# A fused image filter, text transformer and fusion network on one core: neighbour rows by transfers, a freed PSUM bank, norms scaled by ScalarE

## Chip, core and metric

The kernel runs on one core of a Trainium2 chip. Its time is device time in microseconds, the median of some runs. A profile is one execution of the program, recorded by the hardware; its span runs from the first to the last recorded instruction. The engines are TensorE (PE; its weight loads are PEld), VectorE (DVE), ScalarE (ACT), GpSimd (POOL) and the sync engine (SP), which here issues the transfers. Each runs its own instruction stream in order and meets the others at semaphores.

## What is computed

Three parts, all in float32. The first filters eight 256x256 images in ten iterations each, with differences to the right and lower neighbour and back:

```python
u = sigmoid(o / 0.5); q = 0
for _ in range(10):
    q = max(q - 0.5 * ((u_below - u) * vf1 + (u_right - u) * vf0), 0)
    Tq = (vf1*q - above(vf1*q)) + (vf0*q - left(vf0*q))
    u = sigmoid((o - Tq) / 0.5)
image_tokens = (o - Tq) / 0.5          # 256 tokens of 256 features
```

The second is a text transformer: 8 sequences of 128 tokens, width 256, four layers, each with 16-head attention, an output projection, a layer norm, a feed-forward pair 256 to 1024 to 256 with relu, and a second layer norm:

```python
h = layernorm(h + attention(h) @ wc) * g1 + e1
h = layernorm(h + relu(h @ w1 + b1) @ w2 + b2) * g2 + e2
```

The third joins both to 384 tokens per sample and applies windowed attention with a sink to the layer norm of the sum, adds it, then adds spike counts of a squared-relu feed-forward (256 to 1024 to 256) of a second layer norm.

## The kernel before

Engines are programmed by hand: one function per engine, with the order of all work written out, and semaphores between them. There are three stages.

*Text.* Samples go in pairs, so that four layers by four pairs make 16 blocks. `block_step(a, f, it)` runs the attention of block `a` beside the output projection, norm and feed-forward of block `f = a - 1`, and two filter iterations `it` and `it + 1`. `first_step` has attention of block 0 alone and two iterations. In PE's order the block starts with `carry_attn` (the residual put into PSUM by identity matmuls), `scores(a, 0)`, `project_out(f)`, `values(a)`, then `turn_probs`/`attend` in four parts among `ff1(f, 0..3)`, `carry_ffn`, and `ff2` in eight parts. `ff1` (L588) writes each quarter of the hidden layer to the one bank `ps_t[:, 0]`, and waits from the second quarter on until ACT's `hidden_out` has read the quarter before. The norms after `project_out` and `ff2` are `moments_*` (DVE, bn_stats L1557, bn_aggr L1560), `scale_of` (POOL: add epsilon L402, power L404), and `plain_rows` (DVE, two instructions at L1576).

*Fusion.* `fuse_first` handles sample 0 beside the last feed-forward of the text and two iterations; `fuse_step(n)` for n = 1 to 4 runs attention of sample n beside the feed-forward of n - 1 and two or one iteration; `fuse_late(n)` for n = 5 to 7 has no iteration, and `fuse_last` is the feed-forward of sample 7. On DVE are also `copy_text` (L1666), `norm_x` and `norm_y` (three instructions each at L1662) and `values_biased` (L1682).

*The filter iteration.* Two images lie over the 128 partitions, four image rows in each (`u`, `p1`: 4 rows of 256). DVE takes `differences` (L1507 inner rows, L1508 columns, L1511), `last_row` (L1515, L1516), `advance` (L1519, L1520), `flux_cols` (L1526), `flux_rows` (L1523), `inner_divergence` (L1532, L1533) and `divergence` (L1537, L1538, L1539). The row below the fourth and the one above the first lie in the next or the previous partition. PE brings them with a shift matrix: `rows_below` (L469) after ACT's tanh (`filter_out`, L997), `rows_above` (L473) after `flux_rows`. They lie in the PSUM bank `halo`. 32 of the 40 iterations run in the text stage, 8 in the fusion stage.

SP loads the weights of layer l + 1 when the last block of layer l has used the tile, and the images and all fusion weights at the start.

```python
    def ff1(k, j):
        ...
        else:
            pe_.wait_ge(s["act_ff1"], 4 * k + j)
        for m in range(2 * j, 2 * j + 2):
            for c in range(KC):
                last = mm(ps_t[:, 0, D * (m % 2):D * (m % 2) + D], w1[:, c, P * m:P * m + P], hT_f[:, c], ...)
```

## Time and profile before

| | us |
|---|---|
| median of 3 runs | 1062.35 (1060.9 to 1063.59) |
| the profiled execution's own time | 1059.45 |
| its span | 1057.5 |
| start to the end of `first_step` | 57.9 |
| 14 blocks, k = 1 to 14 | 555.9 |
| block 15 | 43.4 |
| `fuse_first` | 53.9 |
| `fuse_step` 1 to 4 | 187.2 |
| `fuse_late` 5 to 7, `fuse_last` | 128.6, 30.6 |

The text stages are cut where DVE ends the second `normalise` of a block (L1553), the fusion stages where PE ends `fuse_values`. A row of a window gives its length, then for each engine the busy time and number of instructions, the granted clock of TensorE as a share of full speed, and the transfers. The busy time of PE is modelled, and cannot be read as the time that its work needs at its peak.

### The profile page before, as it was taken

How to read it: one execution, taken by the hardware profiler on the slowest of the kernel's cores; microseconds unless marked ns; L12 is line 12 of the kernel's file. 1: busy time of each engine (PE TensorE's matmuls, PEld its weight loads, DVE VectorE, ACT ScalarE, POOL GpSimd, SP SyncE). 2: the span in 40 equal slices, each digit the busy share in tenths (PEclk: the TensorE clock that was granted, in tenths of full speed). 3: DMA queues.
4: the chain of work that ended last, by engine and by line, in shares of the span. 5: the costliest groups of instructions: out<-in, count | busy, mean ns of one | idle time of the engine just before them, and what ended most of it. 6: DMA issues, size and time to landing. Idle time of an engine off the chain costs nothing.

```text
span 1057.5 us, 18395 instructions
## 1 busy us (share of the span) xinstructions
PE 945.2 (89%) x6972; PEld 714.7 (68%) x6992; DVE 900.7 (85%) x1318; ACT 636.8 (60%) x2105; POOL 87.9 (8%) x149
## 2 busy tenths in 40 slices
PE   3589999889889989989989988789998999999997
PEld 2367777667667767767767766566666766667675
DVE  4999999999999999999999999798699699543542
ACT  1666667766666666666766665446455564745633
POOL 6100010001010010010010001010000001000000
PEclk9799999999999999999999999999999999999999
DMA  7600000110000110000110000000000000100000
GB/s 162 244 1 2 1 30 6 46 61 1 1 31 11 43 39 21 1 31 11 46 55 2 1 21 2 1 11 2 26 1 26 9 18 1 46 25 2 16 1 30
DMA packets 13544, 28.67 MB, mean 27 GB/s; under 512 B 2704, under 2 KB 9232, under 8 KB 12176
## 3 DMA queue, kind: packets, MB, share of 16 engines
q1 hardware_dynamic: 13072, 26.44, 7.5%
q0 software_dynamic: 384, 1.05, 0.6%
q8 instruction: 56, 0.92, 0.4%
q14 instruction: 32, 0.26, 0.1%
HBM read 22.25 MB, written 5.24 MB: 26 GB/s over the span
## 4 chain that ended last, share of the span: by engine, by line
PE 45%; DVE 43%; ACT 7%; issue 4%; DMA 1%; SPq 0%; POOL 0%; POOLq 0%; ACTq 0%; DVEq 0%
PE ps_t L595 8%; PE ps_t L604 7%; PE ps_s L493 4%; DVE neg_max L1544 4%; PE ps_m L808 3%; PE ps_t L797 3%; DVE f L1538 2%; DVE f L1520 2%; DVE f L1516 2%; DVE f L1519 2%; DVE p L1526 2%; DVE f L1511 2%; DVE p L1523 2%; DVE f L1508 2%; DVE f L1533 2%
## 5 line engine op out<-in xcount | busy, mean ns | idle before, releaser
L1010 ACT ACTIVATE prob<-ps_s,neg_max 128x128 f32<-128x128 f32 x512 | 180.1, 379 | 52.2 <-DVE neg_max L1544 52.2
L595 PE MATMUL ps_t<-hT_f,w 128*128 128x256 f32 x512 | 133.0, 404 | 33.1 <-ACT hT_f L1022 17.2
L595 PEld LDWEIGHTS ps_t<-hT_f,w 128*128 128x128 f32 x512 | 95.3, 196 | 58.9 <-ACT hidT L1076 23.9
L1018 ACT ACTIVATE probT<-ps_t 128x512 f32<-128x512 f32 x128 | 77.2, 603 | 83.2 <-PE ps_t L554 52.6
L604 PE MATMUL ps_t<-w,hidT 128*128 128x256 f32 x512 | 125.4, 383 | 0.0
L1010 ACT ACTIVATION_READ_ACCUMULATOR prob<-ps_s,neg_max 128x1 f32 x512 | 112.8, 220 | 0.0
L604 PEld LDWEIGHTS ps_t<-w,hidT 128*128 128x128 f32 x512 | 91.1, 190 | 12.2 <-issue 3.0
L797 PE MATMUL ps_t<-km,w_fc 128*128 128x384 f32 x256 | 94.4, 504 | 1.7 <-ACT km L1183 1.0
L554 PE MATMUL ps_t<-ident,prob 128*128 128x128 f32 x512 | 81.4, 283 | 5.9 <-ACT prob L1010 3.7
L1076 ACT ACTIVATE hidT<-ps_t,b 128x256 f32<-128x256 f32 x128 | 54.8, 491 | 49.8 <-PE ps_t L595 49.8
L554 PEld LDWEIGHTS ps_t<-ident,prob 128*128 128x128 f32 x512 | 63.0, 145 | 28.4 <-issue 11.8
L1544 DVE TENSOR_REDUCE neg_max<-ps_s 128x8 f32<-128x1024 f32 x64 | 76.0, 1210 | 2.9 <-PE ps_s L544 2.9
L1215 ACT ACTIVATE prob<-ps_s,neg_max 128x128 f32<-128x128 f32 x192 | 54.0, 380 | 29.3 <-DVE neg_max L1688 29.3
L493 PE MATMUL ps_s<-hT_a,w_attn 128*128 128x256 f32 x256 | 65.3, 401 | 3.0 <-ACT hT_a L1022 2.3
L808 PE MATMUL ps_m<-w_pr,o_all 128*128 128x256 f32 x256 | 66.1, 385 | 0.0
L797 PEld LDWEIGHTS ps_t<-km,w_fc 128*128 128x128 f32 x256 | 46.4, 193 | 27.4 <-issue 3.9
L493 PEld LDWEIGHTS ps_s<-hT_a,w_attn 128*128 128x128 f32 x256 | 48.5, 200 | 12.1 <-ACT hT_a L1022 5.1
L1520 DVE TENSOR_TENSOR f<-f 128x1024 f32<-128x1024 f32 x40 | 50.0, 1251 | 1.4
L808 PEld LDWEIGHTS ps_m<-w_pr,o_all 128*128 128x128 f32 x256 | 45.7, 190 | 7.4
L1519 DVE SCALAR_TENSOR_TENSOR f<-f 128x1024 f32<-128x1024 f32 x40 | 49.3, 1231 | 1.1
L1538 DVE TENSOR_TENSOR f<-f 128x1024 f32<-128x1024 f32 x40 | 49.0, 1225 | 1.4
L1516 DVE TENSOR_TENSOR f<-f,vf 128x1024 f32<-128x1024 f32 x40 | 49.0, 1225 | 1.4
(172 smaller groups left out, 1879.3 us busy)
## 6 DMA issues: line engine op xcount, KB each, us to landing
w<-in_w SPq DMA_DIRECT2D x8, 1024.0 KB, 4.9
w_attn<-in_w_attn SPq DMA_DIRECT2D x4, 768.0 KB, 4.6
out<-w SPq DMA_DIRECT2D x7, 384.0 KB, 2.4
o_all<-in_o SPq DMA_DIRECT2D x4, 512.0 KB, 10.5
filtered<-f_out SPq DMA_DIRECT2D x4, 512.0 KB, 2.6
x<-filtered SPq DMA_DIRECT2D x8, 256.0 KB, 2.7
vf<-in_vf SPq DMA_DIRECT2D x4, 256.0 KB
w_attn<-in_w_attn SPq DMA_DIRECT2D x4, 256.0 KB, 3.1
```

The costliest lines, as they stand in the source:

```text
L493: last = mm(dst, w_attn[:, c, D * w + P * m:D * w + P * m + P], hT_a[:, k % 2, c], start=(c == 0), stop=(c == KC - 1))
L554: last = tr(ps_t[:, 1, P * hh:P * hh + P], prob[:, n % 2, 4 * half + hh], ident[:])
L595: last = mm(ps_t[:, 0, D * (m % 2):D * (m % 2) + D], w1[:, c, P * m:P * m + P], hT_f[:, c], start=(c == 0), stop=(c == KC - 1))
L604: last = mm(ps_t[:, 0, D * t:D * t + D], hidT[:, m, P * t:P * t + P], w2[:, m], start=False, stop=(m == MC - 1), skip_group_check=True)
L797: last = mm(ps_t[:, m % 2, 0:TOK], w_fc[:, c, P * m:P * m + P], xn2T[:, c], start=(c == 0), stop=(c == KC - 1))
L808: last = mm(dst, hid_f[:, m, P * t:P * t + P], w_pr[:, m], start=(m == 0), stop=(m == MC - 1))
L1010: last = A(prob[:, n % 2, hh], ps_s[n % 2][:, hh], ACT.Exp, scale=-1.0, bias=neg_max[:, n % 2, hh:hh + 1], accum_out=den)
L1018: A(probT[:, 4 * half:4 * half + 4].rearrange("p h k -> p (h k)"), ps_t[:, 1], ACT.Copy).then_inc(s["act_pT"], 1)
L1516: link(tt(fa, fa, vf[:, 0], ALU.mult))
L1519: link(stt(q_st, q_st, 0.0, fa, ALU.max, ALU.subtract))
L1520: link(tt(q_st, q_st, fb, ALU.subtract))
L1544: dve.tensor_reduce(neg_max[:, n % 2], ps_s[n % 2][:], AX.X, ALU.min).then_inc(s["dve_max"], 1)
```

## The change

The iterations per block become a list: one in block 0 and in block 15, two in the others, so 30 in text; `fuse_first` and all four `fuse_step` have two. `u` gets a fifth row below and `p1` a fifth row above; SP fills them by two SBUF to SBUF transfers each (63 partitions of 1 KB, one per image), and the two PE functions, the shift matrices and the bank `halo` go. The differences across rows become one instruction over 1024 elements, where there had been one of 768 and one of 256. SP's loads are spread through the blocks among these transfers.

The freed bank, `ps_y` (`row_bank`), takes the residual and output projection and `turn_ffn`; `ff1` alternates between it and `ps_t[:, 0]`. The norms are scaled by ACT, as `scale * x + shift`, for which POOL also makes `-mean` and `-mean * rstd` (two small instructions more for each norm). The exceptions are the last layer's second norm and sample 0's first norm, which stay on DVE. ACT also takes `copy_text` and the copy of the window values; the value bias is added in `values_in`. The orders of PE, ACT and DVE are rewritten in all stages: among others the second `head_max` of a block follows `flux_rows`, and `scores(a, 1)` comes behind three quarters of `ff1`.

```diff
-ITERS_IN_BLOCK = 2
-TEXT_ITERS = ITERS_IN_BLOCK * BLOCKS
-FUSE_ITERS = [2, 1, 2, 1, 2, 0, 0, 0]
+BLOCK_ITERS = [1, 2, 2, 2, 2, 2, 2, 2, 2, 2, 2, 2, 2, 2, 2, 1]
+TEXT_ITERS = sum(BLOCK_ITERS)
+FUSE_ITERS = [2, 2, 2, 2, 2, 0, 0, 0]
...
-        u = sb("u", [P, RPP, IMG + 1])
+        u = sb("u", [P, RPP + 1, IMG + 1])
-        p1 = sb("p1", [P, RPP, IMG])
+        p1 = sb("p1", [P, RPP + 1, IMG])
-        halo = ps("halo", [P, 2, IMG])
+        ps_y = ps("ps_y", [P, 2, D])
+        row_bank = ps_y[:, :, :].rearrange("p t n -> p (t n)")
+        ff_banks = [ps_t[:, 0], row_bank]
...
+            def rows_below(it):
+                if it < ITERS * PAIRS:
+                    sp.wait_ge(s["act_tanh"], it + 1)
+                    for at in (0, 64):
+                        sp.dma_start(u[at:at + 63, RPP, 0:IMG], u[at + 1:at + 64, 0, 0:IMG]).then_inc(s["halo_u"], 16)
+
+            def rows_above(it):
+                sp.wait_ge(s["dve_flux"], it + 1)
+                for at in (0, 64):
+                    sp.dma_start(p1[at + 1:at + 64, 0], p1[at:at + 63, RPP]).then_inc(s["halo_p"], 16)
...
+            rows_below(0)
+            for k in range(BLOCKS):
+                it, its, l = sum(BLOCK_ITERS[:k]), BLOCK_ITERS[k], k // PAIRS
+                for i in range(its):
+                    rows_above(it + i)
+                    if i == 0 and k < PAIRS - 1:
+                        load_images(k + 1).then_inc(s["l_img_rest"], 16)
+                    if i == 0 and k % PAIRS == PAIRS - 1 and l + 1 < LAYERS:
+                        load_projections(l + 1)
+                    if i == 0 and k % PAIRS == 0 and l:
+                        load_out(l)
+                    if i == 1 and k % PAIRS == 0 and l:
+                        load_ff_in(l)
+                    rows_below(it + i + 1)
+                    pair_done(it + i)
...
             def scale_attn(k):
-                scale_of(s["dve_stat_a"], s["pool_eps_a"], k, mv_a, var_eps_a, rstd_a, s["pool_rstd_a"])
+                pool.wait_ge(s["dve_stat_a"], k + 1)
+                if k:
+                    pool.wait_ge(s["act_ln1"], k)
+                pool.tensor_tensor(var_eps_a[:], mv_a[:, :, 1], eps_c[:, 0:2], ALU.add).then_inc(s["pool_eps_a"], 1)
+                pool.tensor_tensor(neg_mean_a[:], mv_a[:, :, 0], minus[:, 0:2], ALU.mult).then_inc(s["pool_eps_a"], 1)
+                pool.wait_ge(s["pool_eps_a"], 2 * k + 2)
+                pool.tensor_tensor(rstd_a[:], var_eps_a[:], pow_half[:, 0:2], ALU.pow).then_inc(s["pool_rstd_a"], 1)
+                pool.wait_ge(s["pool_rstd_a"], k + 1)
+                pool.tensor_tensor(shift_a[:], neg_mean_a[:], rstd_a[:], ALU.mult).then_inc(s["pool_shift_a"], 1)
...
-            def rows_below(it):
-                pe_.wait_ge(s["act_tanh"], it + 1)
-                mm(halo[:, 0], up_shift[:], u[:, 0, 0:IMG], start=True, stop=True).then_inc(s["pe_halo"], 1)
...
             def ff1(k, j):
...
-                else:
-                    pe_.wait_ge(s["act_ff1"], 4 * k + j)
+                    if k:
+                        pe_.wait_ge(s["h_ready"], 4 + k)
+                elif j >= 2:
+                    pe_.wait_ge(s["act_ff1"], 4 * k + j - 1)
                 for m in range(2 * j, 2 * j + 2):
                     for c in range(KC):
-                        last = mm(ps_t[:, 0, D * (m % 2):D * (m % 2) + D], w1[:, c, P * m:P * m + P], hT_f[:, c], start=(c == 0), stop=(c == KC - 1))
+                        last = mm(ff_banks[j % 2][:, D * (m % 2):D * (m % 2) + D], w1[:, c, P * m:P * m + P], hT_f[:, c], start=(c == 0), stop=(c == KC - 1))
...
-            def block_step(a, f, it):
+            def block_step(a, f, it, its):
                 carry_attn(f)
                 scores(a, 0)
                 project_out(f)
                 values(a)
-                rows_below(it)
                 turn_probs(a, 0, 0)
                 turn_ffn(f)
                 ff1(f, 0)
                 turn_probs(a, 0, 1)
                 ff1(f, 1)
-                rows_above(it)
+                ff1(f, 2)
+                attend(a, 0)
+                turn_probs(a, 1, 0)
                 scores(a, 1)
...
+            def scaled_rows(k, bank, rstd_, shift_):
+                hp = h[:, 2 * (k % PAIRS):2 * (k % PAIRS) + 2]
+                for t in range(2):
+                    last = A(hp[:, t], bank[:, D * t:D * t + D], ACT.Identity, scale=rstd_[:, t:t + 1], bias=shift_[:, t:t + 1])
+                return last
...
             def block_step(a, f, it, its):
                 exps(a, 0, 0)
-                exps(a, 0, 1)
+                values_out(a)
+                norm_attn(f)
                 probs_out(a, 0, 0)
                 ffn_in(f)
+                exps(a, 0, 1)
+                hidden_out(f, 0)
...
-            def last_row(it):
-                dve.wait_ge(s["pe_halo"], 2 * it + 1)
-                link(stt(fa[:, RPP - 1], halo[:, 0], edge[:], u[:, RPP - 1, 0:IMG], ALU.add, ALU.subtract))
+            def differences_down(it):
+                dve.wait_ge(s["halo_u"], 32 * it + 32)
+                link(tt(fa, u[:, 1:, 0:IMG], u[:, 0:RPP, 0:IMG], ALU.subtract))
                 link(tt(fa, fa, vf[:, 0], ALU.mult))
...
             def divergence(it):
-                dve.wait_ge(s["pe_halo"], 2 * it + 2)
-                link(tt(fa[:, 0], p1[:, 0], halo[:, 1], ALU.subtract))
+                dve.wait_ge(s["dve_flux"], it + 1)
+                dve.wait_ge(s["halo_p"], 32 * it + 32)
+                link(tt(fa, p1[:, 1:], p1[:, 0:RPP], ALU.subtract))
                 link(tt(fa, fa, fb, ALU.add))
                 stt(fa, o_all[:, it // ITERS], 4.0, fa, ALU.mult, ALU.subtract).then_inc(s["dve_div"], 1)
...
-            def block_step(a, f, it):
-                differences(it)
+            def block_step(a, f, it, its):
+                differences_across(it)
                 head_max(a, 0)
                 moments_attn(f)
+                differences_down(it)
+                advance(it)
+                flux_rows(it)
                 head_max(a, 1)
-                norm_attn(f)
-                last_row(it)
-                advance(it)
                 flux_cols(it)
-                flux_rows(it)
-                inner_divergence(it)
+                divergence_across(it)
                 divergence(it)
                 head_max(a, 2)
                 head_max(a, 3)
...
+                if its > 1:
+                    differences_across(it + 1)
+                    differences_down(it + 1)
+                    advance(it + 1)
...
+                if its > 1:
+                    flux_rows(it + 1)
+                    flux_cols(it + 1)
                 reciprocals(a, 0)
...
+                    divergence_across(it + 1)
+                reciprocals(a, 1)
                 moments_ffn(f)
-                reciprocals(a, 1)
-                divergence(it + 1)
-                norm_ffn(f)
+                if its > 1:
+                    divergence(it + 1)
                 normalise(a, 0)
                 normalise(a, 1)
```

## Rows read from the trace of the kernel before

**Rows 1.** The page's first part: busy us, share of the span, instructions.
```profile
PE 945.2 (89%) x6972; PEld 714.7 (68%) x6992; DVE 900.7 (85%) x1318; ACT 636.8 (60%) x2105; POOL 87.9 (8%) x149
```

**Rows 2.** Windows: stretch, length, busy PE, PEld, DVE, ACT, POOL, clock, transfers.
```profile
22.00:57.93 35.93, 23.82 (x167) 16.04 (x166) 32.40 (x34) 20.96 (x86) 8.45 (x13) 0.76 0.56 199
57.93:613.80 555.87, 513.08 (x3648) 405.13 (x3648) 539.84 (x679) 378.29 (x1389) 39.55 (x70) 0.99 0.06 21
613.80:657.23 43.43, 35.16 (x257) 26.84 (x255) 42.47 (x64) 27.51 (x100) 5.46 (x7) 1.00 0.03 11
657.23:711.10 53.87, 45.11 (x370) 34.31 (x373) 46.94 (x82) 22.55 (x57) 6.40 (x9) 0.97 0.02 6
711.10:898.30 187.20, 176.24 (x1416) 124.57 (x1424) 160.47 (x278) 102.67 (x262) 10.48 (x16) 1.00 0.04 12
898.30:1026.90 128.60, 122.10 (x1017) 86.54 (x1026) 57.98 (x139) 70.78 (x188) 5.21 (x10) 1.00 0.06 19
...
296.52:335.68 39.16, 36.12 (x262) 28.54 (x261) 38.25 (x49) 26.83 (x100) 2.82 (x5) 1.00 0.07 21
```

**Rows 3.** Groups by line: shapes, count, busy us, mean ns, idle before.
```profile
L1532 DVE TENSOR_TENSOR f<-p 128x768 f32<-128x768 f32 x40 | 38.3, 957 | 1.2
...
L1507 DVE TENSOR_TENSOR f<-u 128x768 f32<-128x768 f32 x40 | 37.1, 927 | 2.6 <-ACT u L997 2.6
...
L1515 DVE SCALAR_TENSOR_TENSOR f<-halo,edge,u 128x256 f32<-128x256 f32 x40 | 19.0, 475 | 0.0
...
L1022 ACT ACTIVATE hT_f<-ps_t,cols 128x256 f32<-128x256 f32 x32 | 16.3, 560 | 10.7 <-PE ps_t L478 10.7
L1576 DVE TENSOR_SCALAR h<-ps_t,mv_a,rstd_a 128x256 f32<-128x256 f32 x32 | 15.9, 539 | 0.8 <-POOL rstd_a L404 0.2
L1537 DVE TENSOR_TENSOR f<-p,halo 128x256 f32<-128x256 f32 x40 | 15.9, 398 | 0.9 <-PE halo L473 0.3
...
L1662 DVE TENSOR_SCALAR km<-x,mv_x,rstd_x 128x256 f32<-128x256 f32 x24 | 8.4, 407 | 0.1
```

**Rows 4.** Timeline within one steady block: start, duration, engine, line.
```profile
318.58 0.59 PE L469 MATMUL halo<-u,up_shift 128*128 128x256 f32 x2
...
331.52 0.70 POOL L404 TENSOR_TENSOR rstd<-var_eps,pow_half 128x2 f32<-128x2 f32 x1
331.62 1.23 DVE L1538 TENSOR_TENSOR f<-f 128x1024 f32<-128x1024 f32 x1
...
332.88 1.23 DVE L1539 SCALAR_TENSOR_TENSOR f<-o_all,f 128x1024 f32<-128x1024 f32 x1
...
334.02 0.99 DVE L1576 TENSOR_SCALAR h<-ps_t,mv,rstd 128x256 f32<-128x256 f32 x2
334.13 1.06 ACT L997 ACTIVATE u<-f 128x1024 f32<-128x1024 f32 x1
334.93 0.41 DVE L1553 TENSOR_TENSOR attnT<-ps_m,rden 128x256 f32<-128x256 f32 x1
...
335.59 0.94 DVE L1507 TENSOR_TENSOR f<-u 128x768 f32<-128x768 f32 x1
```

**Rows 5.** Transfers: count, KB each, median us from issue to landing.
```profile
w<-in_w SPq DMA_DIRECT2D x8, 1024.0 KB, 4.9
...
x<-filtered SPq DMA_DIRECT2D x8, 256.0 KB, 2.7
...
out<-w SPq DMA_DIRECT2D x1, 128.0 KB, 1.7
```

**Rows 6.** PE's waits in blocks 1 to 14: total us, times, longest.
```profile
PE ps_t L595 <- ACT hidT L1076: 13.6, 26, 0.6
PE ps_t L478 <- DVE h L1576: 10.5, 14, 0.9
```

**Rows 7.** Timeline in `fuse_first`: a POOL instruction and the DVE one beside it.
```profile
674.27 1.04 POOL L419 TENSOR_TENSOR hT_r<-hT_f,cols 128x512 f32<-128x512 f32 x1 [3.46 <-ACT hT_f L1022]
...
674.45 1.95 DVE L1520 TENSOR_TENSOR f<-f 128x1024 f32<-128x1024 f32 x1
```

More of the change, by code:

```diff
@@ L494, in project, with carry @@
                 return last
[L496 removed]
+            def carry(bank, src):
                 for t in range(2):
@@ L1646, in first_step @@
                 reciprocals(0, 0)
-                differences(1)
-                last_row(1)
-                advance(1)
-                flux_cols(1)
-                flux_rows(1)
-                inner_divergence(1)
                 reciprocals(0, 1)
-                divergence(1)
                 normalise(0, 0)
```

734 lines of the change are left out of this document (374 added, 360 removed).

## The prediction

> **What bounds the kernel now.** I read the page's shares first: PE is busy 89% of the span and DVE 85% [rows 1], so the whole page cannot say which of them sets the time. The windows can [rows 2]. In blocks 1 to 14 DVE is busy 539.84 of 555.87 us, 97%; PE 513.08, 92%; ACT 68%. A steady block has 39.16 us with 38.25 of DVE. What is left to DVE there, 0.9 us, is spread over some 49 instructions and is the gap between linked ones. So DVE sets the text stage, and PE, which waits in small pieces for ACT and DVE [rows 6], is close behind it. In `fuse_step` 1 to 4 the order is reversed: PE 176.24 of 187.2 us, 94%, DVE 160.47, 86%. In `fuse_late` PE is busy 95% and DVE 45%: there is room for filter work on DVE in the fusion stage, and none in the text stage. Block 15 (42.47 of 43.43) and `first_step` from 22 us on (32.40 of 35.93) are DVE's too.
>
> **Part 1: rows by transfers, on DVE.** Across rows, 927 + 475 = 1402 ns [rows 3] become one instruction of 1024 elements, about 1225 as L1538 and L1539 take [rows 4]. Back across rows, 957 + 398 = 1355 become 1225. Instructions of which the second does not wait overlap by some 0.06 us, so that of 0.31 us per iteration I count 0.18: 0.36 us per block.
>
> **Part 2: the norms.** DVE loses two pairs of L1576 per block. A pair takes from 334.02 to 334.93, 0.91 us [rows 4]; two make 1.82. ACT gains four instructions of 560 ns, of the form of L1022 (scale and bias from PSUM, the same 128x256) [rows 3], about 2.0 us, on 26.83 of 39.16. That is hidden: the first pair lies where ACT waits for the first maximum and the second behind the queries' copy, before the next exponentials. POOL's two more instructions, each some 0.2 us, lengthen the chain moments to `ff1(f, 0)` by 0.3 to 0.5 us; DVE no longer delays that chain, and ACT may (it must finish four exponentials and the values' copy first). PE's wait for this norm is 0.75 us per block now [rows 6]; I expect 1.2.
>
> **A new wait.** Today L1576 stands between the last divergence and the next differences and covers the tanh. L1539 ends at 334.11, the tanh runs 334.13 to 335.19, and DVE goes on at 335.59 without a gap [rows 4]. After the change only `normalise` stands there, 335.59 - 334.93 = 0.66 us, against 1.1 to 1.2 us from the end of the divergence to the end of the tanh. DVE stalls 0.45 us per block; the first exponentials' maximum is queued behind it, and ACT and PE's `turn_probs` wait for that.
>
> A steady block on DVE: 39.16 - 0.36 - 1.82 + 0.45 = 37.4 us, 1.75 less. 14 blocks: **-24.5 us**.
>
> **Part 3: does PE follow?** PE loses four shift matmuls per block of 0.59 us each [rows 4], 2.4 us, and the wait of `ff1` for `hidden_out`, about 1.0 us [rows 6]. 36.12 - 2.4 = 33.8 busy; with the 5% of idle that `fuse_late`, a PE-bound stage, has [rows 2], 35.5. By the chain instead of the share: 39.16 less 2.4 and 1.0, plus 0.5 for the norm, is 36.3. POOL's `hT_r`, on which `carry_ffn` waits, follows the first divergence (17.8 us into the block by DVE's sum) and takes 1.04 us [rows 7], soon enough for a `carry_ffn` at about 20. So PE lies at 35.5 to 36.3 and DVE stays the bound, by 1 us. The freed bank and the matmuls alone bring nothing in this stage; they are what lets PE follow.
>
> **Part 4: are the transfers hidden?** The trace has no SBUF to SBUF transfer. The nearest rows are 1.7 us from issue to landing for 128 KB and 2.7 for 256 KB; 4.9 for 1 MB is the upper end [rows 5]. SP issues two per halo, some 0.45 us apart, so from the releasing instruction to both landed I take 0.1 + 0.45 + 1.7 to 2.7 = 2.3 to 3.3 us (63 KB is nearest to the 128 KB row); at most 5.5. The covers on DVE: from `flux_rows` to the divergence in the first half `head_max`, `flux_cols` and the differences across, 3.6 us; in the second 3.8; from tanh to `differences_down` in the first half two differences, a maximum and the moments, 4.6 us; in the second half the maxima hide the tanh and 3.6 us remain. All four are longer than 3.3: the transfers cost nothing, and everything beyond 3.6 us would cost up to four times per block. SP's order puts the 1 MB loads right behind a halo, with 8 us or more to the next. SP waits for weights (`pe_v`, `pe_wc`, `pe_ff1`, `pe_ff2`) that are reached before the halo queued behind them.
>
> The Trainium skill speaks against this form: "DMA: Bandwidth & Descriptors", section "Rules for kernel authors", says that two transfers to disjoint partition halves serialize and that one should be used, and its section on the anatomy of a DMA gives a fixed 2.0 us plus bytes at 436 GB/s. If the second waited for the whole of the first, that would be an estimated 4.3 us by the page; the trace of before has no such pair to agree or disagree. What it would do here is the second rival.
>
> **Part 5: the moved iterations.** One iteration is 15 us of DVE. Block 15 has 42.47 us of DVE [rows 2]; less 15, less the norm, it falls to some 26, and PE's 35 decides with its waits: 43.4 to 36.5, **-6.9 us**. `first_step` loses an iteration too, 17 us of DVE remain of 32.4, but its attention chain stays: the second maximum now comes behind `flux_rows`, 6 us later than today, so the exponentials of the second part start later and PE and ACT (23.82 and 20.96 us busy, clock 0.76) are left to run almost in series. The gain lies between 0 and 35.93 - 23.82 = 12 us; I take **-3.5**, near the lower end for that order.
>
> `fuse_first`: DVE loses 0.9 (norm), six instructions of 407 ns (`norm_x`, `norm_y`) [rows 3], some 0.8 (copy and values, two instructions near L1537's 0.4) and 0.4 (rows), so 46.94 becomes 42.4; PE loses four shift matmuls, 2.4, and starts its queries without waiting for block 15's DVE. Of 53.87 I take **-6.0**: 48, which leaves PE (42.7) its present share of waits. Bounds 0 and -9.
>
> `fuse_step` 1 to 4: DVE 160.47 + 2 x 15 - 8 x 0.2 - 4 x 3.3 = 175.7, 43.9 per step; PE 176.24 - 12 x 0.59 = 169.2, 42.3 per step, 44.4 with its 5%. The two are now almost equal, so 45.5 per step: 182 for 187.2, **-5.2**. Bounds -10 and +8. Here the transfers have longer covers, since maxima and normalisations stand between. `fuse_late` and the tail: PE-bound, DVE's work moved to ACT (70.78 of 128.6): 0.
>
> The Trainium skill's page "SBUF — State Buffer", section "SBUF: two separate sides", says that a GpSimd instruction and a DVE instruction with two SBUF inputs hold a shared port pair exclusively. The trace agrees for a large one: L1520 takes 1.95 us beside POOL's hT_r, in place of 1.23 [rows 7, 4]. It does not for a small one: L1538 takes 1.23 beside the power of 0.70 us [rows 4]. If each of the two new small ones cost DVE its 0.2 us, 30 text norms would add 12 us; I count nothing.
>
> **The sum.** -24.5 - 6.9 - 3.5 - 6.0 - 5.2 = -46.1: the span goes from 1057.5 to 1011.4; with 1.95 us around it (1059.45 - 1057.5) 1013.4. That is the profiled execution. The median of the runs shown is 2.9 us above it, so 1016.
>
> **The rivals.**
> 1. *Another engine's order becomes the bound.* The norm goes through ACT, whose order is rigid: when four exponentials are late, `norm_attn`, `turn_ffn` and all of `ff1` are. For it: PE has only 1 us of room, and waits for this norm already. Against: 1.75 us of DVE leave the block. Blocks at 38.5 instead of 37.4: 1016 + 15 = 1031.
> 2. *Slower: the two halves of a halo run one after the other.* 2 x 2.3 = 4.6 us from release to landing, against covers of 3.6: 1.0 us for each of the 60 halos in the text stage, +60: 1076. It decides from 46 / 60 = 0.77 us of stall, at 4.4 us; between 4.2 and 4.4 nothing would change. Against: 16 engines share even 1 MB in 4.9 us, and one small transfer leaves them almost idle. This is what the skill's rule above would bring about.
> 3. *More is gained.* No tanh stall, blocks at PE's 36.2, `first_step` -8, steps at 44: 1016 - 17 - 4.5 - 6 = 988. For it: if the first maximum is not ready, the stall lies in a wait that exists anyway.
> 4. *The moved iterations are not hidden*, `fuse_step` at 48.5 as DVE and PE wait for each other: 1016 + 12 = 1028; it lies in the range.
>
> **Chances and range.** Forecast with its bounds (1000 to 1027) 0.60; rival 1 or 4, alone or together up to 1045, 0.19; rival 3, 0.13; within 0.3% by transfers of 4.2 to 4.4 us, 0.03; rival 2, 0.05. Of measurements I take 0.3% as what can be told from no change. Faster 0.92, same 0.03, slower 0.05. The range goes from rival 3 to rivals 1 and 4 together with a further 0.1 us per block: 986 to 1045.
>
> **What the profile after would show.** Part 1: DVE instructions of 1024 elements at 1.22 us, none of 768, and no wait for a transfer beyond 0.2 us; any idle of DVE before `differences_down` or `divergence` that ends with a landing contradicts part 4. Part 2: `norm` on ACT at about 0.56 us, and a DVE idle of some 0.45 us per block before the differences, ended by the tanh; if it isn't there, rival 3. Part 3: a steady block of 37.4 us with DVE at 36.5 busy, PE below 34.5; if PE's waits for ACT's h have grown over 1.5 us per block, rival 1. Part 5: block 15 near 36.5 us with DVE idle, steps near 45.5 with DVE near 44. The forecast is wrong if the block is not 37.4, since that term is more than half of it.

## The result, and the profile after

| us | before | after |
|---|---|---|
| median of the runs of this comparison | 1061.62 (1060.78 to 1063.59) | 1094.66 (1088.74 to 1100.5) |
| profiled execution, span | 1059.45, 1057.5 | 1100.5, 1098.8 |
| start to the end of `first_step` | 57.9 | 63.2 |
| blocks 1 to 14 | 555.9 | 581.2 |
| block 15 | 43.4 | 43.7 |
| fusion | 400.3 | 410.6 |

The changed kernel is slower: ratio 1.0308, 95% interval 1.0246 to 1.037. I had forecast 1016 us. Every stage misses its forecast: `first_step` by 8.8 us, blocks 1 to 14 by 49.8, block 15 by 7.2, fusion by 21.5. The profiled execution of the changed kernel is the longest of its four, 5.8 us above their median.

The page's first part after, to be held against [rows 1]:

```profile
PE 937.7 (85%) x6808; PEld 717.3 (65%) x6832; DVE 848.9 (77%) x1121; ACT 690.4 (63%) x2221; POOL 177.7 (16%) x244
```

The windows after, for [rows 2] (stretch, length, busy PE, PEld, DVE, ACT, POOL, clock, transfers); the last row is one steady block:

```profile
22.00:63.23 41.23, 23.17 (x167) 16.21 (x166) 18.08 (x20) 22.23 (x89) 6.37 (x13) 0.67 0.28 86
63.23:644.46 581.23, 504.27 (x3535) 402.26 (x3534) 509.98 (x568) 399.42 (x1438) 111.57 (x126) 0.92 0.12 39
644.46:688.18 43.72, 35.37 (x246) 27.21 (x244) 26.63 (x46) 28.11 (x101) 7.15 (x13) 0.87 0.07 22
688.18:1098.80 410.62, 369.79 (x2852) 267.59 (x2876) 285.65 (x466) 236.65 (x589) 40.13 (x69) 0.95 0.06 20
227.85:269.77 41.92, 36.57 (x258) 28.89 (x256) 37.06 (x42) 29.62 (x105) 7.98 (x9) 0.92 0.15 51
```

DVE did lose its work (539.8 to 510.0 us in the 14 blocks) and is now idle for 12% of them. Two columns stand out: POOL, from 39.6 to 111.6 us, far more than 28 times two short instructions; and PE's granted clock, from 0.99 to 0.92. The groups of POOL say where its time is (busy us and mean ns of one, then idle before):

```profile
L456 POOL TENSOR_TENSOR rstd_a<-var_eps_a,pow_half 128x2 f32<-128x2 f32 x16 | 24.8, 1551 | 1.3
L467 POOL TENSOR_TENSOR rstd<-var_eps,pow_half 128x2 f32<-128x2 f32 x16 | 23.2, 1450 | 1.3
L453 POOL TENSOR_TENSOR var_eps_a<-mv_a,eps_c 128x2 f32<-128x2 f32 x16 | 17.2, 1078 | 140.7 <-DVE mv_a L1665 140.7
```

The same instructions in the kernel before:

```profile
L404 POOL TENSOR_TENSOR rstd_a<-var_eps_a,pow_half 128x2 f32<-128x2 f32 x16 | 11.1, 695 | 1.3
L402 POOL TENSOR_TENSOR var_eps_a<-mv_a,eps_c 128x2 f32<-128x2 f32 x16 | 3.1, 195 | 182.3 <-DVE mv_a L1560 182.3
```

One steady block of the changed kernel in order of time shows what they meet (start, duration, then in brackets idle before and who ended it):

```profile
232.72 0.25 DVE L1665 BATCH_NORM_AGGREGATE mv_a<-stats_a 128x2 f32<-128x6 f32 x2
232.89 1.19 DVE L1621 TENSOR_TENSOR f<-u 128x1024 f32<-128x1024 f32 x1
233.05 1.08 POOL L453 TENSOR_TENSOR var_eps_a<-mv_a,eps_c 128x2 f32<-128x2 f32 x1 [5.81 <-DVE mv_a L1665]
234.12 1.25 DVE L1622 TENSOR_TENSOR f<-f,vf 128x1024 f32<-128x1024 f32 x1
234.37 1.55 POOL L456 TENSOR_TENSOR rstd_a<-var_eps_a,pow_half 128x2 f32<-128x2 f32 x1
235.99 0.68 POOL L458 TENSOR_TENSOR shift_a<-neg_mean_a,rstd_a 128x2 f32<-128x2 f32 x1
236.71 1.02 ACT L1095 ACTIVATE h<-ps_y,shift_a,rstd_a 128x256 f32<-128x256 f32 x2 [2.27 <-POOL shift_a L458]
237.79 1.12 PE L539 MATMUL ps_y<-ident,h 128*128 128x128 f32 x4 [3.60 <-ACT h L1095]
240.01 3.70 PE L658 MATMUL ps_t<-hT_f,w 128*128 128x256 f32 x8 [1.11 <-ACT hT_f L1065]
```

`var_eps_a` starts 0.16 us behind the start of L1621, a difference of two SBUF tensors, and ends 0.05 us after it, at 234.13 to 234.08. `rstd_a` starts inside L1622 and still runs for 0.55 of its usual 0.70 us after that one's end at 235.37. `shift_a` starts inside L1625 and ends 0.04 us after it. From the end of the moments to ACT's norm there are 3.7 us. In the kernel before there were 1.15, from 302.20 to 303.35:

```profile
301.95 0.25 DVE L1560 BATCH_NORM_AGGREGATE mv_a<-stats_a 128x2 f32<-128x6 f32 x2
303.35 1.00 DVE L1576 TENSOR_SCALAR h<-ps_t,mv_a,rstd_a 128x256 f32<-128x256 f32 x2
```

Of the 2.6 us between the two, the lengthening of `var_eps_a` and `rstd_a` is 0.88 and 0.86. `shift_a` takes 0.68 where its twin `neg_mean_a`, which starts 0.02 us ahead of L1622, takes 0.19; if that is its own time, 0.5 more is lengthening. That leaves some 0.4 us for the two added instructions themselves. PE stands still for 3.6 us and comes back at its lower level, 1.2 GHz: the first quarter of `ff1` takes 3.70 us, later quarters 1.89. The waits after, total, times, longest, for [rows 6]:

```profile
PE ps_y L539 <- ACT h L1095: 56.3, 16, 3.7
ACT h L1095 <- POOL shift_a L458: 37.8, 16, 3.3
DVE neg_max L1649 <- PE ps_s L605: 59.8, 16, 4.7
DVE f L1614 <- ACT u L1040: 5.5, 12, 0.5
DVE f L1621 <- DMA u<-u: 10.4, 6, 6.5
```

In the kernel before, the first of them was:

```profile
PE ps_t L478 <- DVE h L1576: 11.9, 16, 0.9
```

The longer wait of PE comes back to DVE as a wait for the next scores (59.8 us).

### The profile page after: what moved, and what is told of

The parts are those of the page before. It is cut to its first block, busy times and chain, and to the rows that moved or that the text cites. A ratio compares the mean times of both kernels' runs of the same rounds, so it can differ in the third digit from the quotient of the medians.

```text
span 1098.8 us, 18348 instructions
## 1 busy us (share of the span) xinstructions
PE 937.7 (85%) x6808; PEld 717.3 (65%) x6832; DVE 848.9 (77%) x1121; ACT 690.4 (63%) x2221; POOL 177.7 (16%) x244
## 4 chain that ended last, share of the span: by engine, by line
PE 34%; DVE 34%; ACT 12%; POOL 7%; issue 6%; DMA 4%; SPq 1%; POOLq 0%; ACTq 0%; DVEq 0%
PE ps_t L658 8%; PE ps_t L857 6%; DMA u<-u 4%; PE ps_y L658 3%; PE ps_s L804 2%; ACT u L1040 2%; PE ps_m L868 2%; DVE f L1643 2%; POOL rstd_a L456 2%; DVE f L1622 2%; DVE f L1626 2%; DVE f L1625 2%; DVE f L1621 2%; PE ps_t L615 2%; DVE f L1642 2%
## 5 line engine op out<-in xcount | busy, mean ns | idle before, releaser
L669 PE MATMUL ps_t<-w,hidT 128*128 128x256 f32 x512 | 129.2, 386 | 0.0
L1649 DVE TENSOR_REDUCE neg_max<-ps_s 128x8 f32<-128x1024 f32 x64 | 76.7, 1219 | 59.8 <-PE ps_s L605 59.8
L1053 ACT ACTIVATION_READ_ACCUMULATOR prob<-ps_s,neg_max 128x1 f32 x512 | 121.4, 237 | 0.0
L658 PE MATMUL ps_t<-hT_f,w 128*128 128x256 f32 x256 | 89.7, 512 | 16.8 <-ACT hT_f L1065 16.7
L615 PE MATMUL ps_t<-ident,prob 128*128 128x128 f32 x512 | 85.5, 293 | 17.6 <-ACT prob L1053 16.7
L615 PEld LDWEIGHTS ps_t<-ident,prob 128*128 128x128 f32 x512 | 63.3, 150 | 45.0 <-ACT prob L1053 25.2
L658 PEld LDWEIGHTS ps_t<-hT_f,w 128*128 128x128 f32 x256 | 64.6, 260 | 34.4 <-ACT hT_f L1065 22.3
L539 PE MATMUL ps_y<-ident,h 128*128 128x128 f32 x64 | 16.0, 397 | 56.3 <-ACT h L1095 56.3
L658 PE MATMUL ps_y<-hT_f,w 128*128 128x256 f32 x256 | 63.2, 391 | 0.0
L1305 ACT ACTIVATE prob<-ps_s,neg_max 128x128 f32<-128x128 f32 x192 | 53.9, 382 | 11.3 <-DVE neg_max L1773 11.3
L1772 DVE TENSOR_REDUCE rmax<-ps_s 128x4 f32<-128x512 f32 x48 | 33.0, 687 | 34.1 <-PE ps_s L804 33.8
L464 POOL TENSOR_TENSOR var_eps<-mv,eps_c 128x2 f32<-128x2 f32 x16 | 16.5, 1032 | 260.0 <-DVE mv L1665 260.0
L1621 DVE TENSOR_TENSOR f<-u 128x1024 f32<-128x1024 f32 x40 | 48.4, 1210 | 11.4 <-DMA u<-u 10.4
L1614 DVE TENSOR_TENSOR f<-u 128x1024 f32<-128x1024 f32 x40 | 48.6, 1214 | 5.5 <-ACT u L1040 5.5
```

What stands on the lines that cost most here:

```text
L615: last = tr(ps_t[:, 1, P * hh:P * hh + P], prob[:, n % 2, 4 * half + hh], ident[:])
L658: last = mm(ff_banks[j % 2][:, D * (m % 2):D * (m % 2) + D], w1[:, c, P * m:P * m + P], hT_f[:, c], start=(c == 0), stop=(c == KC - 1))
L669: last = mm(ps_t[:, 0, D * t:D * t + D], hidT[:, m, P * t:P * t + P], w2[:, m], start=False, stop=(m == MC - 1), skip_group_check=True)
L1053: last = A(prob[:, n % 2, hh], ps_s[n % 2][:, hh], ACT.Exp, scale=-1.0, bias=neg_max[:, n % 2, hh:hh + 1], accum_out=den)
L1305: last = A(prob[:, t % 2, head], quad[hb][:, P * hh:P * hh + P], ACT.Exp, bias=neg_max[:, t, head:head + 1])
L1614: link(tt(fb, u[:, 0:RPP, 1:], u[:, 0:RPP, 0:IMG], ALU.subtract))
```

## The experiments

My theory after the traces: POOL's short instructions of the norm are held by DVE's instructions with two SBUF inputs, since the change put those right behind the moments in place of the second maximum, which reads PSUM; the norm of the attention then reaches PE late, and PE's clock falls in the wait. I call this lengthening of POOL's instructions the hold; an exchange is the pair of transfers that brings one set of neighbour rows. The rivals were the late maximum, the norm's place on ACT, the transfers and the moved iterations. Each run was compared with runs of the kernel before made beside it, and its ratio is to those; `e5` and the like are the runs' names, and in the table each row from e2 on adds to the one above. The stages of the profiled runs, in us:

| | first | 1 to 14 | 15 | fusion | ratio of the runs |
|---|---|---|---|---|---|
| before | 57.9 | 555.9 | 43.4 | 400.3 | 1 |
| after | 63.2 | 581.2 | 43.7 | 410.6 | 1.031 |
| e2, maximum ahead | 63.3 | 567.0 | 41.7 | 406.6 | 1.012 |
| e1, and norm on DVE | 63.0 | 552.4 | 40.0 | 408.1 | 1.003 |
| e5, and first exchange early | 55.9 | 550.8 | 39.9 | 405.6 | 0.995 |

**e2: the second maximum directly behind the moments.**

```diff
                 moments_attn(f)
+                head_max(a, 1)
                 differences_down(it)
                 advance(it)
                 flux_rows(it)
-                head_max(a, 1)
```

> The changed kernel with one line moved in DVE's block_step: the second head_max comes directly behind moments_attn, as in the kernel before, ahead of differences_down. It reads PSUM only, so POOL's four small instructions get some 1.2 us in which DVE runs nothing with two SBUF inputs. Theory P (DVE's two-SBUF-input instructions hold POOL up, the norm's chain grows, PE idles and its clock falls): epsilon add of the attention norm back from 1.08 to 0.19 us, power from 1.55 to about 0.7, PE's wait for ACT's h from 3.7 to some 1.5 us per block, granted clock above 0.96, blocks of 38.5 to 39.5 in place of 41.5: 1050 to 1065 us. Rival T (transfers and SP's queue are the cost): nothing of that, 1090 to 1100. Rival O (the rigid order of ACT alone, with POOL's lengthening harmless): POOL's times fall, but the blocks stay above 41.

1078.38 us, ratio 1.0123 (1.0065 to 1.0182). POOL's groups in e2:

```profile
L458 POOL TENSOR_TENSOR shift_a<-neg_mean_a,rstd_a 128x2 f32<-128x2 f32 x16 | 15.3, 959 | 1.3
L456 POOL TENSOR_TENSOR rstd_a<-var_eps_a,pow_half 128x2 f32<-128x2 f32 x16 | 12.0, 748 | 1.3
L453 POOL TENSOR_TENSOR var_eps_a<-mv_a,eps_c 128x2 f32<-128x2 f32 x16 | 4.0, 250 | 140.6 <-DVE mv_a L1665 140.6
```

The two that now run beside a maximum from PSUM are back at 250 and 748 ns, and the one that reaches into the differences behind it has become longer, 959 ns. PE's wait for h falls from 56.3 to 35.4 us. The forecast on POOL held, the one on the time did not: PE still waits 2.2 us a block (forecast 1.5), the clock of the blocks stays at 0.92 (forecast above 0.96), a block takes 40.5 us and the run 13 us more than the top of the range. In one steady block there are still 2.3 us from the end of the moments to ACT's norm. This run moves the maximum too, so it does not part the two causes by its time; POOL's rows do for the port.

**e1: e2, and the attention norm on DVE again**; POOL makes only `rstd_a`, ACT's `norm_attn` is gone.

```diff
                 head_max(a, 1)
+                norm_attn(f)        # on DVE: ts(hp[:, t], rows[:, t], mv_a[:, t, 0:1], rstd_a[:, t:t + 1], ...)
                 differences_down(it)
```

> e2_max_first, and the attention norm of the text stage scaled on DVE again (two instructions behind the second head_max, POOL makes the factor only). P: PE's wait for h as before the change, 0.7 to 1.0 us per block, blocks near 38, clock 0.98: 1040 to 1055. If scaling on ACT as such is the cost, this is faster than e2_max_first by over 10 us; if only POOL's hold-up is, the two are within 5 us, since DVE gets 0.9 us more per block. T: 1090 to 1100.

1066.22 us, ratio 1.0025 (0.9998 to 1.0052); 12 us less than e2, which by my own rule means that scaling on ACT is a cost of its own. The run takes away POOL's `neg_mean_a` and the held `shift_a` together with ACT's norm, so it does not part these. PE's wait for h is 16.9 us, nearly as forecast; the time is above the forecast of 1040 to 1055, since a block takes 39.5 us and not 38.

**e3: the order of the change in the kernel before.**

```diff
+                last_row(it)
                 head_max(a, 1)
                 norm_attn(f)
-                last_row(it)
```

> The kernel before with two lines of DVE's block_step in reverse order: last_row (whose second instruction has two SBUF inputs) between moments_attn and the second head_max. No transfer, no norm on ACT. P: POOL's epsilon add or power for the attention norm, 0.19 and 0.70 us today, grows towards 1 to 1.5 us in every block where it meets L1516, and PE's wait for h grows; the norm itself comes 1.7 us later at most by DVE's order. 1065 to 1090 us. O and T: POOL's times as before, and 1062 to 1070 by the later norm.

1128.27 us, ratio 1.0601 (1.0556 to 1.0645). The time is far above the forecast, and the part on POOL missed: its instructions kept 197 and 696 ns, because nothing stood beside them. DVE waited there for PE's shift matmul:

```profile
328.29 0.25 DVE L1560 BATCH_NORM_AGGREGATE mv_a<-stats_a 128x2 f32<-128x6 f32 x2
328.89 0.69 POOL L404 TENSOR_TENSOR rstd_a<-var_eps_a,pow_half 128x2 f32<-128x2 f32 x1
329.65 0.48 DVE L1515 SCALAR_TENSOR_TENSOR f<-halo,edge,u 128x256 f32<-128x256 f32 x1 [1.11 <-PE halo L469]
332.57 0.99 DVE L1576 TENSOR_SCALAR h<-ps_t,mv_a,rstd_a 128x256 f32<-128x256 f32 x2
```

So the run says nothing on the hold. With that wait of 1.1 us and the two instructions of `last_row`, the maximum and the norm come 2.9 us later (4.0 us from the moments to the norm, for 1.15), and a block takes 44.2 us in place of 39.7: some 1.5 us for each microsecond of lateness.

**e9: the kernel before with the power computed twice**, so that this norm alone comes 0.7 to 0.8 us later.

```diff
+                pool.tensor_tensor(spare_a[:, 0:2], var_eps_a[:, 0:2], pow_half[:, 0:2], ALU.pow)...
                 pool.tensor_tensor(rstd_a[:, 0:2], var_eps_a[:, 0:2], pow_half[:, 0:2], ALU.pow)...
```

> The kernel before with POOL's power for the attention norm computed twice (0.7 us and a handover more, 16 times), so that the norm and only the norm comes 0.8 us later; DVE waits for it. If a late norm costs its delay, 16 x 0.8 = 13 us: 1073 to 1078. If it is amplified (PE's clock falls, and exponentials and scores are late in turn), 1085 to 1100. If the chain has slack, under 1068.

1084.4 us, ratio 1.0192 (1.0154 to 1.0229): 20 us for 16 x 0.8 = 13 us, blocks 41.3. PE's wait for h is 24.2 us (11.9 before), its clock 0.96. That lies between the two forecasts. The lateness of the norm alone, without the maximum, is paid in full and by half again.

**e6: the changed kernel, six matmuls whose result nobody reads in PE's wait for the norm.**

```diff
                 turn_probs(a, 0, 0)
+                if f:
+                    pe_.wait_ge(s["h_ready"], 4 + f)
+                for _ in range(6):
+                    mm(ps_t[:, 0, 0:D], ident[:], hT_a[:, a % 2, 0], start=True, stop=True)
                 turn_ffn(f)
```

> The changed kernel with six matmuls whose result nobody reads (into the free half of ps_t) between turn_probs(a, 0, 0) and turn_ffn, where PE waits 3.7 us per block for the norm. They take some 3 us of that wait. If the lower clock after that wait is a cost of its own (the four matmuls of ff1(f, 0) take 3.7 us after it, 2.0 elsewhere, granted clock 0.92), the clock returns to 0.98 or more, ff1(f, 0) to 2.0 us, and a block loses 1 to 1.7 us: 1070 to 1080. If the clock does not matter beside the chain, 1090 to 1100.

1074.97 us, ratio 1.0108 (1.0077 to 1.0139): 20 us less with more work. Clock in the 14 blocks 0.97 (0.92), and in the block's order:

```profile
233.30 0.66 PE L539 MATMUL ps_y<-ident,h 128*128 128x128 f32 x4 [1.01 <-ACT h L1099]
235.07 2.98 PE L658 MATMUL ps_t<-hT_f,w 128*128 128x256 f32 x8 [1.11 <-ACT hT_f L1069]
```

The same groups took 1.12 and 3.70 us in the changed kernel, 1.2 us more a block, or 18 us in 15 blocks; by the windows the 15 blocks give back 16.3 us. So about half of the loss against before was PE at 1.2 GHz behind a wait in which it did nothing. The rest, 4.6 us by the windows, came in the fusion stage.

**e4: the transfers alone in the kernel before**, with its order of work and its norms; among others:

```diff
-                link(stt(fa[:, RPP - 1], halo[:, 0], edge[:], u[:, RPP - 1, 0:IMG], ALU.add, ALU.subtract))
+                dve.wait_ge(s["halo_u"], 32 * it + 32)
+                link(tt(fa, u[:, 1:, 0:IMG], u[:, 0:RPP, 0:IMG], ALU.subtract))
...
-                link(tt(fa[:, 0], p1[:, 0], halo[:, 1], ALU.subtract))
+                dve.wait_ge(s["halo_p"], 32 * it + 32)
+                link(tt(fa, p1[:, 1:], p1[:, 0:RPP], ALU.subtract))
```

> The kernel before with the first part of the change alone: neighbour rows by two transfers each, one instruction across rows, the two shift matmuls and their bank gone, loads of layers spread among the transfers; images and fusion weights still loaded at the start. P: the transfers are hidden but for the first ones behind the loads, POOL's times as before: 1045 to 1062. T: DVE idles for landings, 1.3 us per block or more: 1080 to 1100.

1124.86 us, ratio 1.0566 (1.0519 to 1.0613), above both forecasts. VectorE's waits in e4:

```profile
DVE f L1582 <- DMA p<-p: 38.6, 33, 1.8
DVE f L1561 <- DMA u<-u: 20.1, 3, 18.7
```

In the order of before only 1.2 us of DVE's work lie between `flux_rows` and the instruction that needs its transfer. The change needs its new order to hide the transfers. 18.7 us is the first exchange alone, issued behind the loads of images and weights.

**e5: e1 with the first exchange issued ahead of the weights.**

```diff
+            sp.wait_ge(s["act_tanh"], 1)
+            for at in (0, 64):
+                sp.dma_start(u[at:at + 63, RPP, 0:IMG], u[at + 1:at + 64, 0, 0:IMG]).then_inc(s["halo_u"], 16)
             sp.wait_ge(s["g_emb"], 16 * (B - 2))
...
-            rows_below(0)
```

> e1_norm_dve with the two transfers of the first halo issued before SP's wait for the gathered rows, ahead of the weight loads. There its first halo landed while the loads ran, and DVE idled 7.3 us for it in first_step. If that wait is first_step's loss, first_step ends 4 to 6 us earlier and nothing else moves: 1060 to 1063 where e1_norm_dve had 1066. Rival: first_step is bound by its attention chain at the low clock, and it gains under 2 us.

1058.56 us, ratio 0.9949 (0.9924 to 0.9973). SP's queue in the changed kernel, and what DVE waits for behind it:

```profile
20.29 0.57 SPq L273 DMA_DIRECT2D w_attn<-in_w_attn  x1
...
22.98 0.43 SPq L278 DMA_DIRECT2D w<-in_w  x1
24.48 1.72 SPq L322 DMA_DIRECT2D u<-u  x2
...
33.21 1.23 DVE L1621 TENSOR_TENSOR f<-u 128x1024 f32<-128x1024 f32 x1 [6.54 <-DMA u<-u]
```

The exchange is issued behind six loads of weights, and DVE can go on only 8.7 us after SP began to issue it. e5 is the only version with all of the work in it that is ahead of the kernel before, by 0.5% (0.3 to 0.8), a small gain; it is 3% ahead of the changed kernel. `first_step` ends 7.1 us earlier than in e1, a little more than forecast.

**e8: e1 with the old distribution of the iterations**; the second iteration also goes back into `first_step` on DVE and ACT.

```diff
-BLOCK_ITERS = [1, 2, 2, 2, 2, 2, 2, 2, 2, 2, 2, 2, 2, 2, 2, 1]
-FUSE_ITERS = [2, 2, 2, 2, 2, 0, 0, 0]
+BLOCK_ITERS = [2] * 16
+FUSE_ITERS = [2, 1, 2, 1, 2, 0, 0, 0]
```

> e1_norm_dve with the iterations as before the change: two in each of the 16 blocks, 2, 1, 2, 1, 2 in the fusion steps. Prediction's part 5: first_step 3 to 8 us longer (a part of that is the late first halo in both), block 15 5 to 7 longer, the two steps with one iteration 1 to 3 us shorter each: 1072 to 1080 against 1066. Rival: the fusion stage pays for the moved iterations in full, and the time is within 0.3% of e1_norm_dve.

1066.79 us, ratio 1.0029 (1.0004 to 1.0053), e1 had 1066.22. Block 15 takes 43.8 us (40.0 in e1), the four fusion steps 189.6 (195 to 196 with all ten iterations; 184.9 before), `first_step` 2.7 more. These steps, and those of e10, are cut where DVE ends the second moments of a sample, and not as in the table before the change. The rival holds: the moves cancel. The two iterations are 6 us of the fusion steps' loss; the other 4.7 us, 189.6 against 184.9, are there without them, and no run here shows their cause.

**e10: e5 with the fusion stage's norms on DVE again**, at the places of the kernel before.

```diff
                 advance(it + 1)
+                norm_x(n + 1)
                 residual(n)
```

> The kernel of e5 with the two norms of the fusion stage back on VectorE, at the places where the kernel before has them. Fusion took 400.3 us before and 405.6 in e5, with two more filter iterations in it. Theory N (ScalarE stands still for GpSimd's shift_y and shift_x, 15.1 and 8.8 us in all in the changed kernel, and this is what fusion lost): fusion 400 to 403, 3 to 6 us less than e5, about 1053 to 1056. Theory I (the two added iterations are the loss; VectorE takes some 1.2 us more a norm and has no room in the steps with two iterations): fusion 405 to 412, 1058 to 1065.

1066.34 us, ratio 1.0046 (1.0012 to 1.008): fusion 412.7 us, a step 51.1 us instead of 48.8. That is theory I's side, 1 us above its bounds. Here the change's norm on ACT is right, by some 7 us.

**e7: each exchange as one transfer of 127 partitions; e11: of 126.**

```diff
-                for at in (0, 64):
-                    sp.dma_start(p1[at + 1:at + 64, 0], p1[at:at + 63, RPP]).then_inc(s["halo_p"], 16)
+                sp.dma_start(p1[1:128, 0], p1[0:127, RPP]).then_inc(s["halo_p"], 16)
```

> The kernel of e5 with each neighbour-row exchange as one transfer of 127 partitions in place of two of 63 (the row at the border between the two images is then wrong: the edge value is overwritten by the other image's row; all else is computed). SP took 0.72 us to issue each half, so the second half of every exchange started 0.72 us behind the first, and in e1's steady block VectorE waited 0.70 us for p<-p and 1.02 us for u<-u. Theory T (the second half ends what VectorE waits for, and VectorE is the bound of a block now): 0.7 us less at each wait that is there, 1.0 to 1.4 us a block, blocks 39.4 -> 38.2 to 38.6, in all 14 to 20 us less than e5: 1039 to 1045. Theory R (these waits lie beside TensorE's path, which ends the block): the waits shrink and the blocks stay within 0.3 us, 1054 to 1058.

> The kernel of e7 with 126 partitions in its one transfer in place of 127 (besides the row at the border between the two images, the last partition's neighbour row is not brought either; all else is computed). In e7 the one transfer of 127 rows was the slow thing: from the last flux instruction to its arrival 7.2 us (two halves of 63: 3.0 us), and while VectorE waited the DMA share was 0.06, one of 16 engines, at 17 GB/s. Theory D (127 rows can't be dealt out evenly, so one DMA engine carries them all; 126 can, over 9 or 14 engines): the one transfer takes 2.3 to 2.6 us, the waits of e5 (0.71 and 1.09 us in a block) shrink to about 0 and 0.4 us, blocks 39.4 -> 38.4, 1038 to 1047. Theory B (crossing partition 64, or the larger size, is slow in itself): as e7, 1300 us or more. If theory D holds for the transfer but TensorE ends the blocks: 1052 to 1057.

e7 took 1354.69 us, ratio 1.2742 (1.266 to 1.2825), e11 1051.66, ratio 0.9889 (0.9832 to 0.9945). The first two rows are waits of e7, the third a window of e7 in which DVE waits for u<-u:

```profile
DVE f L1632 <- DMA p<-p: 198.2, 40, 6.1
DVE f L1611 <- DMA u<-u: 92.4, 20, 4.9
...
431.90:436.61 4.71, 4.71 (x39) 3.60 (x38) 0.08 (x2) 1.73 (x10) 0.00 (x0) 0.93 0.06 17
```

The share is the mean over 16 DMA engines, so 0.06 is what one of them gives when it alone is busy. Counted from the end of the instruction that releases it, not from the later one that I had used in e11's text, the 127 rows took 8.4 us, the two halves 3.1 in e5, the 126 rows 2.6. e7's time is in neither of its two ranges. e11 decides for theory D, with the time as if PE ended the blocks. The waits of e5:

```profile
DVE f L1635 <- DMA p<-p: 10.5, 15, 0.7
DVE f L1614 <- DMA u<-u: 1.1, 1, 1.1
```

The wait for p<-p, 0.7 us in a block of e5, becomes 0.2; blocks go from 39.3 to 38.7. The wait for u<-u of some 1 us, which the texts of e7, e11 and e12 take for one of every block, stands in e5's trace only once.

**e12: the second half of u's rows issued by ACT**, after each tanh (the helper is written out here); SP issues the first half only.

```diff
                     A(u[:, 0:RPP, 0:IMG], fa, ACT.Tanh, scale=0.25).then_inc(s["act_tanh"], 1)
+                    act.wait_ge(s["act_tanh"], it + 2)
+                    act.dma_start(u[64:127, RPP, 0:IMG], u[65:128, 0, 0:IMG]).then_inc(s["halo_u"], 16)
```

> The kernel of e5 with the second half of the rows of u issued by ScalarE, directly behind the tanh that makes them, while SyncE issues the first half. Theory T (the second half lands last because SyncE needs 0.72 us for each issue, and VectorE waits for it): VectorE's wait for u<-u of 1.09 us falls to 0.4 us, 0.7 us a block, some 10 us in all: 1046 to 1051. Theory R (ScalarE's 0.7 us for the issue, 31 times, delays what TensorE waits for): no gain or a loss, 1057 to 1068.

1078.86 us, ratio 1.0132 (1.0077 to 1.0188), 20 us more than e5: theory R, and stronger than it. There was no 0.7 us a block to gain, as said above, and the issue holds ACT for 0.74 us right ahead of the copy of the queries; PE's waits for that copy grow from 10.8 to 19.7 us, those for hT_r from 16.6 to 28.6.

**e13, e14, e15: four of the ten full-width DVE instructions of each iteration narrowed**, in the kernel before, in e5 and in the changed kernel:

```diff
-                tick(tt(fb, fb, vf[:, 1], ALU.mult))
+                tick(tt(fb[:, :, 0:32], fb[:, :, 0:32], vf[:, 1, :, 0:32], ALU.mult))
```

> The kernel before with four of the ten full-width VectorE instructions of each filter iteration (the two products with the vector field, q_st - fb, fa + fb) narrowed from 256 to 32 columns: the filter's result is then wrong, the transformer's part is computed in full. VectorE loses 4 x 1.0 us an iteration, 8 us in a block: 38.25 of 39.16 us busy becomes about 30. Premise P (the one my prediction rests on: VectorE bounds a block, and TensorE, 36.1 us busy, follows): blocks 39.7 on the mean -> 36.5 to 37.5, 15 blocks some 35 to 45 us shorter, 1005 to 1025. Rival F (TensorE's path with its waits for ScalarE and for the norms is as long as VectorE's; block 15 of e5 took 39.9 us with VectorE 27.6 us busy): blocks 38.5 to 39.7, 1045 to 1062.

> The kernel of e5 with the same four instructions narrowed. Premise P: blocks 39.3 -> 36 to 37.5, 1005 to 1020. Rival F: blocks 38.8 to 39.9, 1045 to 1058; then no saving on VectorE could have brought a block under about 39 us.

> The changed kernel with the same four instructions narrowed. Its text norm still goes through GpSimd's four instructions and ScalarE. If the chain over GpSimd (3.6 us in a block, 1 us before) sets its blocks: 41.5 -> 40 to 41.5, 1075 to 1095, though VectorE has 8 us less to do in each. If VectorE's queue sets them: 36 to 38, 1020 to 1040. With fewer long VectorE instructions beside GpSimd's, var_eps_a and rstd_a (1.08 and 1.55 us) may get shorter too.

1045.56, 1011.07 and 1056.95 us; ratios 0.986 (0.9808 to 0.9913), 0.9536 (0.9489 to 0.9584), 0.9957 (0.9933 to 0.9981). A block on the mean of 14: 40.1, 37.1 and 39.8 us. One steady block of each, in this order:

```profile
294.38:334.57 40.19, 37.56 (x261) 29.61 (x261) 31.50 (x49) 26.88 (x100) 2.83 (x5) 0.96 0.07 21
```

```profile
278.22:315.62 37.40, 35.17 (x254) 28.40 (x253) 30.08 (x43) 27.51 (x102) 4.46 (x7) 0.95 0.12 36
```

```profile
299.92:340.24 40.32, 36.41 (x254) 29.33 (x253) 28.92 (x41) 28.47 (x104) 6.11 (x9) 0.92 0.10 33
```

In the kernel before, a block with 7 us less of DVE is no shorter (40.1, before 39.7): rival F. DVE now waits for PE, whose clock in the blocks is 0.97 where it was 0.99, so that a part of the 40.1 us may be the clock. What e13 gained lies outside the 14 blocks (5.1 us in `first_step`, 3.5 in block 15, 10.8 in fusion). In e5 the narrowed block is 2.3 us shorter, 37.1: premise P holds there. In the changed kernel it is at 39.8, 2.7 us above that of e14. These 2.7 us are what the late norm and the late maximum together make of PE's path; the other 1.7 of its 41.5 come when DVE's work lies beside it. e15's time is below its first range. POOL's rows of e15:

```profile
L453 POOL TENSOR_TENSOR var_eps_a<-mv_a,eps_c 128x2 f32<-128x2 f32 x16 | 17.2, 1078 | 142.0 <-DVE mv_a L1665 142.0
L456 POOL TENSOR_TENSOR rstd_a<-var_eps_a,pow_half 128x2 f32<-128x2 f32 x16 | 11.1, 694 | 1.3
```

```profile
306.38 0.32 DVE L1622 TENSOR_TENSOR f<-f,vf 128x128 f32<-128x128 f32 x1
306.63 0.69 POOL L456 TENSOR_TENSOR rstd_a<-var_eps_a,pow_half 128x2 f32<-128x2 f32 x1
306.73 1.23 DVE L1625 SCALAR_TENSOR_TENSOR f<-f 128x1024 f32<-128x1024 f32 x1
```

`var_eps_a` starts inside L1621, which kept its width, and kept its 1078 ns. `rstd_a` starts inside L1622, which was narrowed, and is back from 1551 to 694 ns, though the wide L1625 with two SBUF inputs runs beside it from 0.10 us after its start. The order of work is the same in both kernels. So what holds a small POOL instruction is the DVE instruction that runs when it starts, and not one that starts behind it.

## Why the prediction was wrong, point by point

**What bounds the kernel.** That DVE sets the text stage was wrong, or half the truth. It was read from a share of 97%. e13 shows that the path over PE, with its waits for ACT and for the norm, is as long. The sentence that the freed bank brings nothing by itself is in doubt for the same reason: a light block falls to 37.1 us in e5, with its new orders and two banks (e14), and stays at 40.1 in the old kernel (e13). No run has the bank by itself, so its part in this is open.

**Part 1** held. The DVE instructions of 1024 elements take 1.22 us.

**Part 2**, DVE's share, held: with one norm back on it (0.99 us) e5 does 37.3 us in a block, so without it 36.3 to 36.4, as forecast (36.5; 36.4 after). ACT's two activations take 1.02 us (forecast 1.1). The step that failed is "POOL's two more instructions, each some 0.2 us, lengthen the chain by 0.3 to 0.5 us": it grew by 2.6 us, and PE's wait from 0.75 to 3.5 us a block where I had 1.2. The two instructions themselves are about the 0.4 us of the forecast; what I had at nothing is the hold by DVE, some 2.2 us by the estimate above. I had weighed the shared port only for what POOL costs DVE, and had a row in which a power took 0.70 us beside L1538 [rows 4]; it had begun 0.10 us ahead of it. I never asked what DVE costs POOL, though [rows 7] had the collision in view and the diff put five instructions with two SBUF inputs where a PSUM read had stood. The Trainium skill's page "SBUF — State Buffer", section "SBUF: two separate sides", says that the hold is exclusive and that whichever of the two starts first makes the other wait. Where DVE starts first, e2 and e15 agree, with 1078 and 250 ns, 1551 and 694 ns. Where a small POOL instruction starts first, L1538 [rows 4] and L1625 in e15 kept their 1.23 us.

**The new wait** for the tanh was there as forecast, 0.45 us (5.5 us over 12).

**Part 3.** PE's floor by e14 is 37.1 us against 35.5 to 36.3. I took PE's busy time at full clock and a share of idle from another stage; in the changed kernel the clock was 0.92.

**Part 4.** In the steady blocks it nearly held: 3.1 us for a pair of halves, in my 2.3 to 3.3. In the changed kernel itself DVE waits for u<-u 10.4 us in all, 6.5 of them at the first exchange, and no wait for p<-p is listed. In e5 the cost is 0.7 us a block, and not nothing, since only 2.4 us of work cover the transfer once the maximum stands elsewhere. The step that failed is "SP's order puts the 1 MB loads right behind a halo": the first exchange stands behind the initial loads, 6.5 us, and 7 to 8 us by e5 against e1. SP needs 0.72 us for each half, where I had 0.45. Rival 2, halves in series, did not come: 3.1 us is not 4.6. The rule of the Trainium skill behind it ("DMA: Bandwidth & Descriptors", "Rules for kernel authors") says that the two serialize and that one transfer is better. Here one beat two by 0.5 us with 126 rows, and lost by 5.3 us with 127. The page's 2.0 us and 436 GB/s, from which I had estimated 4.3 us, stand there for transfers issued by GpSimd; these are issued by SP.

**Part 5.** Block 15 gave 3.5 us where it could (e1), not 6.9: with DVE 27.6 us busy it still takes 40, PE's path again. `fuse_step` took 49 us and not 45.5: rival 4 in part. With the old distribution it is still 47.4 (e8), against 46.2 before by the same cut. `fuse_first` took 55.3 us and not 48 (53.9 before), with the clock at 0.85.

**The rivals.** Rival 1, another engine's order, names the place that failed (ACT's norm, then `turn_ffn`, then `ff1`) but prices it at 1.1 us a block; it was 4.1. Of these, 2.2 are gone in e5 (39.3 us a block), where norm and maximum are back at their places; the other 1.9 stay. e11 gives back 0.6 of them with shorter transfers; how the rest came about no run says. In no rival was POOL the one that is late. None priced a fallen clock, though [rows 2] show 0.76 where PE waits much.

The account of the 41 us between the spans: 5.3 in `first_step` (first exchange), 25.3 in blocks 1 to 14, 0.3 in block 15, 10.3 in fusion. In e2 and e6 the same fusion code takes 406.6 and 406.0 us in place of 410.6; the difference lies in `fuse_first` and the start of the next step (688.18 to 770.8), where the clock is 0.86 and theirs is 0.93. So 4 of the 10.3 us are not the fusion stage's own work. In the blocks e2 takes 14 back, e1 15 more. How much of e2's 14 is the maximum and how much the port, its time does not say; e9 gives 1.5 us for each microsecond of the norm by itself.
